# First attention of a four-layer decoder: softmax denominators moved by transfers into 128 rows of 32, and the first key and query slot loaded with the third group

## The chip, the core and the metric

The kernel runs on one core of a Trainium2 chip. The metric is the device time of one execution in microseconds (us), and the time before is the median of three runs. The core has TensorE for matrix products (PE in the views; its weight loads are PEld), VectorE (DVE), ScalarE (ACT), GpSimd (POOL) and SyncE (SP). SP computes nothing here: it issues transfers (DMAs), which the 16 DMA engines carry out. Queue q1 in the views holds the transfers that SP issues, q0 those that POOL issues.

## The reference

The reference is four layers, each an attention over a context of the same 4096 tokens and then a feed-forward block. The change touches the first attention, its preparation, and the stage that combines the first experts and prepares the second attention. With 64 batches of 64 tokens, width 256, and 8 heads of 8 rows, the first attention is

```python
qk = jnp.einsum('bdm,bdn->bmn', qh, kh) * scale
sm = jax.nn.softmax(qk, axis=-1)
ret = jnp.einsum('bmn,bcn->bcm', sm, vh)
x = x + jnp.tanh(g_xattn[0]) * _L0_xattn_ref(_layernorm(x, axis=-1), ctx_2048, ctx_2048)
```

so that the softmax runs over 256 columns of each (batch, head) pair, and its division is by one sum per row.

## The kernel before

The program is a sequence of blocks; at the end of a block all engines wait for each other. Four parts matter.

**Front** (`phase_front`). The context and x are handled in NG = 4 groups of 8 tiles of 128 tokens. For each group q, k and the normalised k are split into three bf16 pieces and stored to DRAM (`k_pieces`, `q_pieces`, `n_pieces`). SP issues these stores in order, waiting before each for the engine that made the piece. With the last group SP also loads four weight matrices (`fr_sq`), which PE transposes and ACT copies, and stores them as `turned`. At its end, SP loads slots 0 and 1 of the first attention.

**Slots** (`Slots`). A slot holds the pieces of two tiles, q and k. There are four slots; a slot's q or k is six DMAs of 768 KB in all.

**First attention** (`phase_attend` with `with_max`, the stage "a0"). It runs over 32 tiles t and 8 heads h. For tile t + 2 and head h, PE's `scores` writes the scores into one of two banks of `psM`, and DVE's `maxima` reduces the bank to row maxima (`mx`). Items (heads, and one extra per tile) take the banks in turn, and PE waits for `ring_read` before it writes a bank again. The extra item stands after head 1 of tile t + 2: `turn_and_gather(t)` transposes the maxima of tile t + 1 into the bank and, with `gather`, brings numerators and denominators of tile t - 2 into it. DVE's `shift_and_divide` then negates the maxima into two bf16 rows (`sh`), inverts the denominators (L1272, 128 x 256) and multiplies (L1274). SP's `shift(t + 1)` waits for `shift_ready` and moves `sh` in four DMAs (L1075) into two extra rows of the q slot, so that the product of q and k in `scores_t` already holds the subtraction. PE waits for all of them at head 0 of tile t + 1:

```python
if h == 0:
    if with_max:
        pe.wait_ge(shift_loaded[t % 2], 64 * (t // 2 + 1))
```

`scores_t` writes `psS` (three banks), ACT takes the exponential of each half (L1237), `values` multiplies with the context into `psV`, ACT copies that out (`ov`, L1223), and POOL adds the scaled result `res` to x. POOL also issues 36 stores of zeros to the DRAM tensor `rows_in`, one after `lay_values(t)` of each tile t, and the last five together at t = 31. After `shift(t + 1)`, SP loads q or k of a slot (L941) and, each second tile, two tiles of values (`ctl`, L1067). The semaphores of one tile and the next use alternate buffers.

**Combine** (`phase_combine_split`). In 8 groups of four tiles the expert outputs are weighed by ACT (L3374), added, normalised and split; SP loads the rows, stores the pieces, and between these loads all four slots of the second attention: k of slot i with step i of 0 to 3, q of two slots each in steps 4 and 5.

## Time and profile before

| What | us |
|---|---|
| median of three runs (lowest, highest) | 3649.17 (3646.26, 3651.99) |
| profiled execution, time | 3641.4 |
| profiled execution, span from first to last instruction | 3639.7 |
| front, from the start of the span to the first product of the first attention | 144.5 |
| first attention, from there to the first instruction of the block behind | 144.5 to 574.7 |

The span is what the trace can divide up; the profiled execution's own time is 1.7 us above it, and 7.8 us under the median. The mean granted clock of TensorE over the span is 0.887 of full speed. All times of rows are counted from the start of the span.

### The profile page before, as it was taken

Reading aid. Unit: us, or ns where it says so; the run is one execution under the profiler, and the core shown is the slowest. Engines: PE = TensorE matmul, PEld = TensorE weight load, DVE = VectorE, ACT = ScalarE, POOL = GpSimd, SP = SyncE. Lnnn points to the kernel's source line nnn. Section 1 sums busy time; section 2 is a strip of 40 time slices with the busy share of each in tenths; the row PEclk is TensorE's granted clock in tenths of the full one; section 3 lists DMA queues with packets and bytes.
Section 4 is the critical chain, followed back from the end, with each engine's and each line's share of the span. In section 5 each row is a group of like instructions: output and inputs, shape, how many; then the busy total and the mean of one; then the engine's idle time right before and its main releaser. Section 6 shows DMA issues by size and latency. Waiting matters only on the chain. (4 is left out here: it accounts for less than half of the span.)

```text
span 3639.7 us, 60306 instructions
## 1 busy us (share of the span) xinstructions
PE 2865.4 (79%) x20178; PEld 1830.7 (50%) x20178; DVE 2155.6 (59%) x4946; ACT 1480.0 (41%) x3032; POOL 1110.8 (31%) x1494
## 2 busy tenths in 40 slices
PE   5488884466699995579947798999989749999993
PEld 4233333222355553433323486454568638888782
DVE  7699993577577776634468687888868620000003
ACT  5377772155222223579935454222245211112120
POOL 3211110277233335512279542000034441111110
PEclk7599996599899998579968899999989669999996
DMA  7766643299422224858500341000044221112204
GB/s 255 204 117 119 119 103 139 91 366 363 166 81 81 79 82 123 201 97 118 101 1 1 123 150 56 1 1 1 1 141 143 92 63 57 50 54 65 72 28 139
DMA packets 261609, 386.10 MB, mean 106 GB/s; under 512 B 56865, under 2 KB 188942, under 8 KB 261056
## 3 DMA queue, kind: packets, MB, share of 16 engines
q1 hardware_dynamic: 236160, 314.07, 32.3%
q0 software_dynamic: 25152, 68.22, 5.4%
q8 instruction: 167, 2.74, 0.3%
q14 instruction: 130, 1.06, 0.1%
HBM read 227.49 MB, written 160.24 MB: 107 GB/s over the span
## 5 line engine op out<-in xcount | busy, mean ns | idle before, releaser
L3167 POOL DMA_INDIRECT rows_out<-e_out,e_tr_dest x224 | 235.5, 1051 | 870.8 <-DVE e_out L3804 504.4
L3804 DVE COPY e_out<-e_psD 128x512 f32<-128x512 f32 x40 | 27.7, 692 | 492.3 <-PE e_psD L3772 492.1
L1237 ACT ACTIVATE a_pt<-a_psS 128x512 f32<-128x512 f32 x512 | 277.6, 594 | 102.0 <-PE a_psS L1133 97.7
L1259 DVE TENSOR_REDUCE a_mx_sb<-a_psM 128x4 f32<-128x1024 f32 x256 | 293.2, 1213 | 9.2 <-PE a_psM L1116 8.2
L3572 PE MATMUL e_psG<-e_wgu,e_yT 128*128 x576 | 275.1, 600 | 25.9 <-ACT e_yT L3600 23.3
L1147 PE MATMUL a_psV<-a_pt,a_vt 128*18 128x256 f32 x4096 | 291.1, 386 | 1.2 <-issue 0.8
L3772 PE MATMUL e_psD<-e_w,e_hT 128*128 128x256 f32 x1280 | 289.9, 386 | 0.0
L3761 PE MATMUL e_psH<-e_yT,e_w 128*128 128x256 f32 x1280 | 284.9, 381 | 1.6 <-issue 0.8
L3704 ACT ACTIVATE e_hT<-e_psH 128x512 f32<-128x512 f32 x160 | 95.6, 597 | 452.6 <-PE e_psH L3761 452.6
L3761 PEld LDWEIGHTS e_psH<-e_yT,e_w 128*128 128x128 f32 x1280 | 244.4, 191 | 35.7 <-issue 2.1
L3772 PEld LDWEIGHTS e_psD<-e_w,e_hT 128*128 128x128 f32 x1280 | 245.5, 194 | 33.3
L1244 ACT ACTIVATE a_pt<-a_psS 128x1024 f32<-128x1024 f32 x256 | 241.6, 1043 | 10.7 <-PE a_psS L1133 9.9
L3606 ACT ACTIVATE e_th<-e_gcap 128x256 f32<-128x256 f32 x144 | 60.0, 417 | 332.4 <-DVE e_ucl L3640 332.4
L1133 PE MATMUL a_psS<-a_q_first,a_k_first 48*128 48x256 bf16 (+1 forms) x1536 | 144.2, 280 | 30.0 <-PEq L119 10.3
L3637 DVE TENSOR_TENSOR e_gub<-e_psG,e_bgu 128x512 f32<-128x512 f32 x144 | 99.3, 690 | 108.6 <-PE e_psG L3572 99.5
L1470 PE MATMUL kv_psK<-e_bgu,e_bd 128*128 128x512 f32 x256 | 127.8, 647 | 32.0 <-DMA e_bd<-ctxT 32.0
L3589 PE MATMUL e_psO<-e_wd,e_hT 128*128 x576 | 149.4, 382 | 2.4 <-ACT e_hT L3612 1.6
L3572 PEld LDWEIGHTS e_psG<-e_wgu,e_yT 128*128 128x128 f32 x576 | 98.9, 192 | 100.1 <-issue 99.9
L1147 PEld LDWEIGHTS a_psV<-a_pt,a_vt 128*18 128x18 f32 x4096 | 86.4, 97 | 108.9 <-issue 68.5
L2858 POOL DMA_INDIRECT rows_in<-sc_y,sc_i x128 | 129.2, 1009 | 38.5 <-issue 37.6
L1043 POOL TENSOR_TENSOR xs<-xs,a_res 128x256 f32<-128x256 f32 x64 | 46.3, 725 | 257.8 <-DVE a_res L1274 257.7
L1133 PEld LDWEIGHTS a_psS<-a_q_first,a_k_first 48*128 48x128 bf16 (+1 forms) x1536 | 54.7, 95 | 127.8 <-ACT a_pt L1244 53.7
(433 smaller groups left out, 6221.1 us busy)
## 6 DMA issues: line engine op xcount, KB each, us to landing
kbd<-e_bgu SPq DMA_DIRECT2D x64, 512.0 KB, 4.6
cr_kbd<-kbd SPq DMA_DIRECT2D x64, 512.0 KB, 3.4
rows_in<-zeros POOLq DMA_DIRECT2D x36, 522.0 KB, 6.3
e_xin<-rows_in SPq DMA_DIRECT2D x144, 128.0 KB
vbd<-e_bd SPq DMA_DIRECT2D x64, 272.0 KB, 4.0
cr_vbd<-vbd SPq DMA_DIRECT2D x64, 272.0 KB, 2.6
cq_rows<-rows_out SPq DMA_DIRECT2D x32, 512.0 KB, 12.1
e_w<-in_L_ffn_w_dram SPq DMA_DIRECT2D x16, 1024.0 KB, 7.6
```

The costliest lines, as they stand in the source:

```text
L1133: ins = pe.matmul(psS[:, (first + b) % S_BANKS, k * DIM:(k + 1) * DIM], at_tile("k", rows(b, KR), t, h, slice(k * P, (k + 1) * P)), at_til ...
L1147: ins = pe.matmul(psV[32 * q:32 * q + 2 * V, b, :], vt[:, t % 4, 2 * k + b, g, q, :], pt[:, probs(t, 4 * g + q), b, k, :], start=(g == 0 a ...
L1237: act.activation(pt[:, probs(t, h), b, :, :], psS[:, unit(t, h, b) % S_BANKS, :].rearrange("p (k c) -> p k c", k=KC), ACT.Exp, scale=scale ...
L1244: act.activation(pt[:, probs(t, h), :, :, :], psS[:, first:first + 2, :].rearrange("p b (k c) -> p b k c", k=KC), ACT.Exp, scale=scale).th ...
L1259: dve.tensor_reduce(mx[:, t % 2, :, h, :], psM[:, k % 2, :, :].rearrange("p b (f c) -> p b f c", f=2), AX_X, ALU.max).then_inc(ring_read, 1)
L1470: ins = pe.matmul(self.psK[:, u, :], self.ct[:, i % 4, k, :], self.w[:, layer, k, :], start=(k == 0), stop=(k == KC - 1))
L2858: pool.indirect_dma_start(out=rows_in[:, :], out_offset=bass.IndirectOffsetOnAxis(ap=index[u][:, k:k + 1], axis=0), in_=y[:, u, :], in_off ...
L3167: pool.indirect_dma_start(out=self.rows_out[0:limit, :], out_offset=bass.IndirectOffsetOnAxis(ap=self.dest[:, t:t + 1], axis=0), in_=rows, ...
L3572: ins = pe.matmul(psG[:, u, :], yT[:, u, k, :], wgu[:, e, k, :], start=(k == 0), stop=(k == KC - 1))
L3589: ins = pe.matmul(psO[:, u, 0:D], hT[:, u, k, :], wd[:, e, k, :], start=(k == 0), stop=(k == KC - 1))
L3761: ins = pe.matmul(psH[:, b, (f % 2) * R:(f % 2 + 1) * R], w1s[:, m, k, f * P:(f + 1) * P], yT[:, u, :, k, :], start=(k == 0), stop=(k == K ...
L3772: ins = pe.matmul(psD[:, u, tt * D:(tt + 1) * D], hT[:, u, f, tt * P:(tt + 1) * P], w2s[:, m, f, :], start=(f == 0), stop=(f == FC - 1))
```

## The change

It has three parts.

1. **First attention.** The maxima are laid out so that one transpose (32 x 128) takes the place of two (16 x 128). `sh` has 32 rows of 128 then, and `shift` needs eight DMAs where it had four. `gather` brings numerators only (two products for four), and ACT copies them to `numer`. The denominators stand in four rows per half of `ov`: `move_sums`, two DMAs, spreads them over 128 rows of 32 (`sums`), DVE inverts 128 x 32, `move_inverses`, one DMA, brings them into 16 rows of 256 (`inverse`), and one product with a matrix of ones and zeros (`repeat`) repeats each over its 8 rows. DVE multiplies. The inverse is taken one tile later than before (`INVERT_LAG`), the scaling two (`SCALE_LAG`), so two more extra items stand at the end.
2. **Front.** Slot 0 is loaded after the third group's stores, slot 1 at the start of the attention. Of the last group's normalised pieces two are stored by ACT, and so are the four `turned` matrices.
3. **Combine.** Only slots 0 and 1 are loaded there, q and k together in steps 6 and 7; slots 2 and 3 are loaded in the second attention.

```diff
+                    if g < NG - 1:
+                        for piece, n_done in enumerate((n_hi, n_mid, n_lo)):
+                            sp.wait_ge(n_done, g + 1)
+                            store_normal(sp, g, piece)
+                    if g == NG - 2:
                         for operand in ("q", "k"):
                             slots.load(sp, operand, 0)
-                    for piece, n_done in ((0, n_hi), (1, n_mid), (2, n_lo)):
-                        sp.wait_ge(n_done, g + 1)
-                        sp.dma_start(n_pieces[g, :, :, PIECES - 1 - piece].rearrange("b h d t c -> (b h) d (t c)"),
-                                     np[:, piece, :, :].rearrange("p t c -> p (t c)")).then_inc(n_stored, 16)
-                for m, (_, dst) in enumerate(pairs):
-                    sp.wait_ge(w_copied, m + 1)
-                    sp.dma_start(dst.rearrange("(k p) o -> p k o", p=P), wt[:, m, :, :]).then_inc(w_stored, 16)
-                for operand in ("q", "k"):
-                    slots.load(sp, operand, 1)
+                sp.wait_ge(n_lo, NG)
+                store_normal(sp, NG - 1, 2)
                 sp.wait_ge(ct_stored, 16 * NG)
                 for u in range(2):
                     sp.wait_ge(k_stored[u], 16 * n_store * (NG // 2))
...
+                act.wait_ge(n_hi, NG)
+                store_normal(act, NG - 1, 0)
+                act.wait_ge(n_mid, NG)
+                store_normal(act, NG - 1, 1)
+                act.wait_ge(w_copied, n_w)
+                for m, (_, dst) in enumerate(pairs):
+                    act.dma_start(dst.rearrange("(k p) o -> p k o", p=P), wt[:, m, :, :]).then_inc(w_stored, 16)
                 act.wait_ge(tanhed, 1)
...
-                        pool.wait_ge(ring_read, turn_item(t + LEAD) + 1)
+                        pool.wait_ge(ring_read, turn_item(t + SCALE_LAG) + 1)
...
-                                         sh[HEADS * b:HEADS * (b + 1), t % 2, s, :]).then_inc(shift_loaded[t % 2], 16)
-
+                            for f in range(2):
+                                rank = PAIR * f + HEADS * b
+                                sp.dma_start(at_tile("q", slice(row, row + 1), t, slice(0, HEADS), slice(f * P, (f + 1) * P)),
+                                             sh[rank:rank + HEADS, t % 2, s, :]).then_inc(shift_loaded[t % 2], 16)
+
+                def move_sums(t):
+
+                    sp.wait_ge(out_done, t + 1)
+                    if t >= 2:
+                        sp.wait_ge(inverted, t - 1)
+                    half = P // 2
+                    for g in range(2):
+                        row = V * g + HD
+                        sp.dma_start(sums[half * g:half * (g + 1), t % 2, :], ov[row:row + 97:32, t % 2, :, :]).then_inc(sums_moved, 16)
+
+                def move_inverses(t):
+
+                    sp.wait_ge(inverted, t + 1)
+                    if t >= 2:
+                        sp.wait_ge(turned, t - 2 + SCALE_LAG + 2)
+                    sp.dma_start(inverse[:, t % 2, :], rec[:, t % 2, :]).then_inc(inverses_moved, 16)
+
+                for s in range(slots.early, 2):
+                    slots.load(sp, "q", s)
+                    slots.load(sp, "k", s)
                 load_values(0)
-                load_values(1)
-                if slots.early < BUFS:
-                    slots.load(sp, "q", 2)
                 if with_max:
                     shift(0)
-                if slots.early < BUFS:
+                load_values(1)
+                slots.load(sp, "q", 2)
+                if with_max:
                     sp.wait_ge(ones_set, 1)
-                    slots.load(sp, "k", 2)
+                slots.load(sp, "k", 2)
                 for t in range(TILES):
                     if with_max and t + 1 < TILES:
                         shift(t + 1)
+                    if with_max and t >= INVERT_LAG:
+                        move_inverses(t - INVERT_LAG)
+                    if with_max and t >= LEAD:
+                        move_sums(t - LEAD)
                     s = t // 2 + 3
-                    if slots.early <= s < NS:
+                    if s < NS:
                         if s >= BUFS:
                             last = SLOT_TILES * (s - BUFS) + SLOT_TILES - 1
                             for b in range(2):
                                 sp.wait_ge(st_done[b], HEADS * (last + 1))
-                        elif t % 2:
-                            sp.wait_ge(ones_set, s - slots.early + 1)
+                        elif with_max and t % 2:
+                            sp.wait_ge(ones_set, s - 1)
                         slots.load(sp, "k" if t % 2 else "q", s)
                     if t % 2 == 0 and t // 2 + 2 < NS:
                         load_values(t // 2 + 2)
                     if t == 20 and prelude is not None:
                         prelude.load(sp)
+                if with_max:
+                    for t in range(TILES, TILES + INVERT_LAG):
+                        move_inverses(t - INVERT_LAG)
+                        if t < TILES + LEAD:
+                            move_sums(t - LEAD)
...
                         pe.wait_ge(ring_read, k - 1)
+                    if copies_before(k - 2):
+                        pe.wait_ge(numer_copied, copies_before(k - 2))
...
                     pe.wait_ge(ring_read, item(t, HEADS - 1) + 1)
-                    for f in range(2):
-                        ins = pe.transpose(bank[0:PAIR, f * P:(f + 1) * P], mx[:, t % 2, :, :, f].rearrange("p b h -> p (b h)"), core.ident[:, :])
-                    return ins
-
-                def gather(t, out):
...
 
+                def repeat_inverses(t, out):
+
+                    pe.wait_ge(inverses_moved, 16 * (t + 1))
+                    return pe.matmul(out, repeat[:, :, :, :].rearrange("r b h d -> r (b h d)"), inverse[:, t % 2, :], start=True, stop=True)
+
                 def turn_and_gather(t):
 
                     k = turn_item(t)
                     pe.wait_ge(ring_read, k - 1)
+                    if copies_before(k - 2):
+                        pe.wait_ge(numer_copied, copies_before(k - 2))
                     if t + 1 < TILES:
                         ins = turn_max(t + 1, psM[:, k % 2, 0, :])
-                    if 0 <= t - LEAD:
-                        ins = gather(t - LEAD, psM[:, k % 2, 1, :])
+                    if 0 <= t - LEAD < TILES:
+                        ins = gather(t - LEAD, psM[:, k % 2, 1, :], 1)
+                    if 0 <= t - SCALE_LAG:
+                        ins = repeat_inverses(t - SCALE_LAG, psM[:, k % 2, 0, DIM:])
                     ins.then_inc(turned, 1)
 
...
                     if t >= 2:
                         act.wait_ge(turned, t - 2 + LEAD + 2)
+                        if with_max:
+                            act.wait_ge(sums_moved, 32 * (t - 1))
                     act.activation(ov[:, t % 2, :, :], psV[:, :, :], ACT.Copy).then_inc(out_done, 1)
+
+                def copy_numer(t):
+                    act.wait_ge(turned, t + LEAD + 2)
+                    if t >= 4:
+                        act.wait_ge(ring_read, turn_item(t - 4 + SCALE_LAG) + 1)
+                    act.activation(numer[:, t % 4, :], psM[:, turn_item(t + LEAD) % 2, 1, 0:DIM], ACT.Copy).then_inc(numer_copied, 1)
...
-                def shift_and_divide(t):
-                    k = turn_item(t)
+                    dve.tensor_tensor(res[:, t % 2, :], psN[:, 0, :], rec[:, t % 2, :], ALU.mult).then_inc(scaled, 1)
+
+                def shift_and_scale(t):
+                    bank = psM[:, turn_item(t) % 2, 0, :]
                     dve.wait_ge(turned, t + 2)
                     if t + 1 < TILES:
-                        shifts(t + 1, psM[:, k % 2, 0, :])
-                    if 0 <= t - LEAD:
-                        divide(t - LEAD, psM[:, k % 2, 1, 0:DIM], psM[:, k % 2, 1, DIM:2 * DIM], ring_read)
+                        shifts(t + 1, bank)
+                    u = t - SCALE_LAG
+                    if u >= 0:
+                        if u >= 2:
+                            dve.wait_ge(added, u - 1)
+                        dve.wait_ge(numer_copied, u + 1)
+                        dve.tensor_tensor(res[:, u % 2, :], numer[:, u % 4, :], bank[:, DIM:2 * DIM], ALU.mult).then_inc(ring_read, 1)
                     else:
                         dve.wait_ge(shift_ready, t + 2)
                         dve.sem_inc(ring_read, 1)
+                    u = t - INVERT_LAG
+                    if 0 <= u < TILES:
+                        dve.wait_ge(sums_moved, 32 * (u + 1))
+                        if u >= 2:
+                            dve.wait_ge(inverses_moved, 16 * (u - 1))
+                        dve.reciprocal(rec[:, u % 2, :], sums[:, u % 2, :]).then_inc(inverted, 1)
 
                 dve.memset(psV[:, :, :], 0.0).then_inc(cleared, 1)
...
-                    if i < slots.early:
-                        slots.load(sp, "k", i)
-                    if i in (4, 5):
-                        sp.wait_ge(stored[i % 2], 16 * PIECES)
-                        for s in range(2 * i - 8, 2 * i - 6):
-                            slots.load(sp, "q", s)
+                    if i == 4:
+                        sp.wait_ge(stored[0], 16 * PIECES)
+                    if 0 <= i - 6 < slots.early:
+                        slots.load(sp, "q", i - 6)
+                        slots.load(sp, "k", i - 6)
                     if 0 <= i - 3:
                         store(i - 3, 1, mid)
                     if 0 <= i - 2 < NG:
...
         with ExitStack() as c:
-            slots = Slots(core, c, "a0", q_pieces, k_pieces, 2)
...
             held = ExitStack()
-            slots = Slots(core, held, "a1", q_pieces, n_pieces, Slots.BUFS)
```

How the order moves, at three places. On DVE, one tile in the middle of the first attention, before (`a_mx_sb` are the row maxima, `a_sh_sb` is `sh`):

```order
L1259 TENSOR_REDUCE a_mx_sb<-a_psM 128x2x2 x8
L1264 TENSOR_SCALAR a_sh_sb<-a_psM 16x256
L1266 SCALAR_TENSOR_TENSOR a_sh_sb<-a_psM,a_sh_sb 16x256
L1272 RECIPROCAL a_rec<-a_psM 128x256
L1274 TENSOR_TENSOR a_res<-a_psM,a_rec 128x256
```

and with the change:

```order
L1334 TENSOR_REDUCE a_mx_sb<-a_psM 128x4 x8
L1339 TENSOR_SCALAR a_sh_sb<-a_psM 32x128
L1341 SCALAR_TENSOR_TENSOR a_sh_sb<-a_psM,a_sh_sb 32x128
L1361 TENSOR_TENSOR a_res<-a_numer,a_psM 128x256
L1370 RECIPROCAL a_rec<-a_sums 128x32
```

The eight reductions stay; the reciprocal has an eighth of its columns and stands behind the multiplication. On SP, what is issued for one tile with an even number, before:

```order
L1075 DMA a_q_rest<-a_sh_sb 1x8x256 x4
L941 DMA a_q_first<-q_pieces 8x8x512
L941 DMA a_q_first<-q_pieces 16x8x512
L941 DMA a_q_first<-q_pieces 24x8x512
L941 DMA a_q_first<-q_pieces 8x8x512
L941 DMA a_q_first<-q_pieces 16x8x512
L941 DMA a_q_first<-q_pieces 24x8x512
L1067 DMA a_ctl<-ctxT 128x2x256
```

and with the change:

```order
L1101 DMA a_q_rest<-a_sh_sb 1x8x128 x8
L1119 DMA a_inverse<-a_rec 16x8x32
L1112 DMA a_sums<-a_ov_sb 64x1x32 x2
L949 DMA a_q_first<-q_pieces 8x8x512
L949 DMA a_q_first<-q_pieces 16x8x512
L949 DMA a_q_first<-q_pieces 24x8x512
L949 DMA a_q_first<-q_pieces 8x8x512
L949 DMA a_q_first<-q_pieces 16x8x512
L949 DMA a_q_first<-q_pieces 24x8x512
L1091 DMA a_ctl<-ctxT 128x2x256
```

Eleven DMAs now stand for the four, and the slot loads behind them. On PE, the extra item and what surrounds it, before:

```order
L1147 MATMUL a_psV<-a_pt,a_vt 18x256 x4
L1116 MATMUL a_psM<-a_k_first,a_q_first 128x256 x4
L1154 MATMUL a_psM<-ident,a_mx_sb 16x128 x2
L1161 MATMUL a_psM<-a_ov_sb,a_pick 64x256 x4
L1133 MATMUL a_psS<-a_q_rest,a_k_rest 128x256 x4
```

and with the change:

```order
L1203 MATMUL a_psV<-a_pt,a_vt 18x256 x4
L1172 MATMUL a_psM<-a_k_first,a_q_first 128x256 x4
L1209 MATMUL a_psM<-ident,a_mx_sb 32x128
L1215 MATMUL a_psM<-a_ov_sb,a_pick 64x256 x2
L1222 MATMUL a_psM<-a_inverse,a_repeat 128x256
L1189 MATMUL a_psS<-a_q_rest,a_k_rest 128x256 x4
```

Four instructions in the place of six, the last one with a wait for `move_inverses`.

## Rows read from the trace of the kernel before

**Rows 1.** Windows: busy us (instructions) per engine, TensorE clock, DMA share, GB/s.
```profile
106.00:144.50 38.50, 8.03 (x35) 6.21 (x36) 15.32 (x8) 10.09 (x10) 0.04 (x1) 0.63 0.95 274
...
200.00:529.00 329.00, 281.32 (x3676) 105.05 (x3676) 317.23 (x318) 243.06 (x453) 52.41 (x108) 1.00 0.60 113
```

**Rows 2.** Reciprocals and SP's issues: ns min/median/max; or busy us, mean ns.
```profile
L1272 DVE RECIPROCAL a_rec<-a_psM x32: 1734/1735/1759, 197.3 to 570.0; 128x256 f32<-128x256 f32 x32
...
L2750 DVE RECIPROCAL s_den<-s_den 128x32 f32<-128x32 f32 x1 | 0.4, 353 | 0.0
...
L1075 SPq DMA_DIRECT2D a_q_first<-a_sh_sb x64: 634/640/1385, 157.7 to 497.9; - x64
```

**Rows 3.** Timeline of one tile: start us, us, engine, line, [idle before, releaser].
```profile
294.29 0.39 PE L1154 MATMUL a_psM<-ident,a_mx_sb 128*16 128x128 f32 x2 [0.42 <-DVE a_mx_sb L1259]
...
295.74 0.41 DVE L1264 TENSOR_SCALAR a_sh_sb<-a_psM 16x256 bf16<-16x256 f32 x1 [0.38 <-PE a_psM L1161]
...
296.53 1.74 DVE L1272 RECIPROCAL a_rec<-a_psM 128x256 f32<-128x256 f32 x1
...
296.63 2.70 SPq L1075 DMA_DIRECT2D a_q_first<-a_sh_sb  x4
...
298.64 9.13 DVE L1259 TENSOR_REDUCE a_mx_sb<-a_psM 128x4 f32<-128x1024 f32 x8
...
299.43 3.78 SPq L941 DMA_DIRECT2D a_q_first<-q_pieces  x6
...
303.93 0.38 PE L1133 MATMUL a_psS<-a_q_first,a_k_first 50*128 50x256 bf16 x4
...
308.15 0.41 DVE L1264 TENSOR_SCALAR a_sh_sb<-a_psM 16x256 bf16<-16x256 f32 x1 [0.38 <-PE a_psM L1161]
```

**Rows 4.** DMA issues: KB each, median us from issue to landing.
```profile
cr_bq<-in_L_xattn_bq_dram SPq DMA_DIRECT2D x2, 0.5 KB, 2.2
```

**Rows 5.** Timeline near the end of the first attention, around its last zeros.
```profile
529.65 2.98 POOL L430 DMA_DIRECT2D rows_in<-zeros  x4
...
532.64 16.65 SPq L1075 DMA_DIRECT2D a_q_rest<-a_sh_sb  x8
...
540.96 0.39 PE L1133 MATMUL a_psS<-a_q_rest,a_k_rest 50*128 50x256 bf16 x4 [0.85 <-DMA a_q_rest<-a_sh_sb]
...
545.73 0.41 DVE L1264 TENSOR_SCALAR a_sh_sb<-a_psM 16x256 bf16<-16x256 f32 x1 [4.21 <-PE a_psM L1161]
```

**Rows 6.** DMA queues from 534 to 537 us: packets, MB, share; no other queue listed.
```profile
q0 software_dynamic: 263, 0.99, 101.7%
```

**Rows 7.** Windows around that stall: columns as in rows 1.
```profile
539.00:542.00 3.00, 1.50 (x24) 0.42 (x16) 2.52 (x3) 2.06 (x5) 0.00 (x0) 1.00 0.05 14
542.00:545.00 3.00, 2.96 (x20) 1.13 (x22) 0.00 (x0) 1.55 (x3) 0.00 (x0) 0.60 0.00 0
```

**Rows 8.** Timeline of the front's end.
```profile
117.27 1.97 PE L304 MATMUL fr_psN<-ident,fr_sq 128*128 128x128 f32 x16 [2.75 <-DMA fr_sq<-in_L_xattn_w_o_dram]
...
123.22 2.29 DVE L391 TENSOR_TENSOR fr_np<-fr_kn,fr_np 128x2048 bf16<-128x2048 f32 x1 [1.98 <-ACT fr_np L317]
...
140.88 2.98 SPq L941 DMA_DIRECT2D a_k_first<-k_pieces  x6
```

**Rows 9.** Timeline of ACT in the combine: the square roots of groups, and a wait.
```profile
1489.23 0.28 ACT L3381 ACTIVATE cq_nrm<-cq_psS 128x128 f32<-128x128 f32 x1 [1.21 <-PE cq_psS L3356]
...
1503.54 0.28 ACT L3381 ACTIVATE cq_nrm<-cq_psS 128x128 f32<-128x128 f32 x1 [1.21 <-PE cq_psS L3356]
...
1520.88 1.06 ACT L3399 ACTIVATE cq_parts<-cq_z_sb 128x1024 bf16<-128x1024 f32 x1 [6.87 <-DMA q_pieces<-cq_parts]
...
1540.45 0.26 ACT L3381 ACTIVATE cq_nrm<-cq_psS 128x128 f32<-128x128 f32 x1
```

**Rows 10.** Timeline of the first attention's last instructions.
```profile
566.90 0.60 ACT L1223 ACTIVATE a_ov_sb<-a_psV 128x512 f32<-128x512 f32 x1 [3.81 <-PE a_psV L1147]
...
572.33 0.72 POOL L1043 TENSOR_TENSOR xs<-xs,a_res 128x256 f32<-128x256 f32 x1 [1.40 <-DVE a_res L1274]
```

More of the change, by code:

```diff
@@ L250, in _ @@
                                    pattern=[[HD, H]], channel_multiplier=-1).then_inc(sel_made, 1)
-                for m in range(slots.early):
+                for m in range(slots.held_first):
                     pool.memset(slots.of("k", m), 1.0).then_inc(ones_set, 1)
@@ L919, in __init__ @@
         self.loaded = [core.lasting_sem(f"{name}_ql{m}") for m in range(self.BUFS)]
-        self.hold(ctx, "first", range(early), "right")
+        self.hold(ctx, "first", range(held_first), "right")
     def hold(self, ctx, part, slots, side=None):
@@ L963, in phase_attend @@
     shift_loaded = [core.sem(f"{n}_sl{m}") for m in range(2)]
-    turned, ring_read, shift_ready, hi_done = (
-        core.sem(n + k) for k in ("_tu", "_rr", "_sr", "_hi"))
+    turned, ring_read, shift_ready, hi_done, sums_moved, inverses_moved, numer_copied = (
+        core.sem(n + k) for k in ("_tu", "_rr", "_sr", "_hi", "_sm", "_im", "_nc"))
     exp_done, pv_done, out_done, gathered, v_laid, made, cleared, gated, inverted, scaled, added, ones_set = (
@@ L1002, in turn_item, with copies_before @@
             return item(TILES - 1, HEADS - 1) + 1 + t + LEAD - TILES
+        def copies_before(k):
+            return sum(1 for t in range(LEAD, TILES + LEAD) if turn_item(t) <= k)
         def unit(t, h, b):
@@ L1016, in _ @@
                 if with_max:
-                    for m in range(slots.early, BUFS):
+                    for m in range(2, BUFS):
                         pool.memset(slots.of("k", m), 1.0).then_inc(ones_set, 1)
@@ L1152, in turn_max, with gather @@
                     pe.wait_ge(ring_read, item(t, HEADS - 1) + 1)
-                    for f in range(2):
-                        ins = pe.transpose(bank[0:PAIR, f * P:(f + 1) * P], mx[:, t % 2, :, :, f].rearrange("p b h -> p (b h)"), core.ident[:, :])
-                    return ins
-                def gather(t, out):
+                    return pe.transpose(bank[0:2 * PAIR, 0:P], mx[:, t % 2, :, :, :].rearrange("p f b h -> p (f b h)"), core.ident[:, :])
+                def gather(t, out, parts):
                     pe.wait_ge(out_done, t + 1)
-                    for d in range(2):
+                    for d in range(parts):
                         for b in range(2):
@@ L1207, in _ @@
                 if with_max:
-                    turn_and_gather(TILES)
-                    turn_and_gather(TILES + 1)
+                    for t in range(TILES, TILES + SCALE_LAG):
+                        turn_and_gather(t)
                 else:
                     pe.wait_ge(scaled, TILES - 1)
-                    gather(TILES - 1, psN[:, :, :].rearrange("p d c -> p (d c)")).then_inc(gathered, 1)
+                    gather(TILES - 1, psN[:, :, :].rearrange("p d c -> p (d c)"), 2).then_inc(gathered, 1)
             @block.scalar
@@ L1245, in _ @@
                                            ACT.Exp, scale=scale).then_inc(exp_done, 2)
+                        if with_max and t >= LEAD and h == 2:
+                            copy_numer(t - LEAD)
                         if with_max and t and h == HEADS - 1:
@@ L1303, in _ @@
                             if h == 1:
-                                shift_and_divide(t)
-                    shift_and_divide(TILES)
-                    shift_and_divide(TILES + 1)
+                                shift_and_scale(t)
+                    for t in range(TILES, TILES + SCALE_LAG):
+                        shift_and_scale(t)
                 else:
```

60 lines of the change are left out of this document (38 added, 22 removed).

## The prediction

> **What bounds the kernel now.** I read the windows by stage first, then the timeline of the stage that the change rewrites, then the waits at its borders. In the first attention's steady part DVE is busy 317.23 of 329.00 us, PE 281.32 and ACT 243.06 [rows 1], so DVE is the limit. The timeline shows how closely. One tile takes from 295.74 to 308.15, 12.41 us: 2.90 for the two shift instructions, the reciprocal and the multiplication, then eight reductions in 9.13, then 0.38 in which DVE waits for PE's extra item [rows 3]. I call the start of the shift instructions T, and the start of `scores_t` for head 0 of the next tile S; here S = 303.93 = T + 8.19, and from S to the next T it is 4.22 [rows 3]. Behind DVE stands a second chain which now has slack: the shift rows. SP starts to issue them at T + 0.89, its four DMAs take 2.70 [rows 3], and a small DMA lands 2.2 after its issue [rows 4]. So they land at about T + 5.2, some 3 us before S.
>
> Outside this loop three places matter. The front ends with DMAs: DVE's last instruction ends at 125.5, SP issues until 143.9, at a DMA share of 0.95 [rows 1, 8]. Behind the first attention's last values POOL's last addition ends at 573.05 [rows 10]. In the combine, the square roots stand 14.31 apart, and then two steps take 36.91 together, in which ACT waits 6.87 for a store that SP could not issue earlier [rows 9].
>
> **The loop: what DVE gains.** The nearest row for 128 x 32 is 0.353 us, against 1.735 for 128 x 256: 1.38 saved [rows 2]. The two shift instructions have half the columns; they save at most 0.4 together, I take 0.25. PE's extra item gets shorter: from 294.29 to T it took 1.45, for two transposes and four products; now it is one transpose, two products and one more product, so I count the 0.38 wait as 0.1. DVE alone would need 12.41 - 1.38 - 0.25 - 0.3 = 10.5 per tile, and would want S at T + 6.5.
>
> ACT gains a copy of 128 x 256, under the 0.60 of the 128 x 512 copy [rows 10], and was busy 243 of 329; it has room.
>
> **The loop: what the shift rows then cost.** They are eight DMAs now, with 8 rows each as before. The row for the old ones is narrow, 634 to 640 ns for most [rows 2], and four took 2.70, so one starts 0.69 after the other. Half the bytes in each need not make an issue shorter; I take 0.69 (0.50, as for six slot loads in 2.98 [rows 8], is the other bound). The last starts 7 x 0.69 = 4.8 after the first. With the first at T + 0.65 and 2.2 to land, PE may start S at T + 7.7: 1.2 later than DVE would want it. So the chain T, eight issues, landing, S, next T becomes the limit: 7.7 + 4.2 = 11.9. From S to T I take the row's 4.22. It could be 3.6, because ACT's 0.60 copy no longer stands in front of the exponentials; it was 4.77 where PE ran at its lower clock (540.96 to 545.73 [rows 5]). Bounds from these rows are 11.3 and 12.5.
>
> SP's queue behind the shift rows matters too. `move_inverses` and `move_sums` are three more DMAs, 2.1 us, then six slot loads that took 3.78 in this tile [rows 3]. With the shift rows that is 5.5 + 2.1 + 3.8 = 11.4 us of SP's time per tile, before it waits for the next `shift_ready`; it just fits. But the slot loads, which began at T + 3.7, now begin near T + 8.2, so their data still move when the next shift rows are issued. I add 0.2 for that. The tile is then 12.1, 0.3 less than now. The trace has 28 such steps (the first reciprocal at 197.3 [rows 2], T of tile 30 at 545.73 [rows 5]): **-8.4**, and -0.8 for the stall at 540.96, which goes from there. Sums and inverses are needed a tile after they are issued; they stay hidden behind 12 us until the end.
>
> **The last zeros.** POOL lays the values of tile t + 1 and issues its zeros behind the addition of tile t - 4, which now waits for the extra item of tile t, not of t - 2. So the last five zeros are issued some 2.5 us after T of tile 30 (behind the multiplication and POOL's 0.72); before, they began ahead of T of tile 29. What they do to shift rows is in the trace: zeros from 529.65, shift rows issued from 532.64, and PE gets them at 540.96, 11.3 after the zeros [rows 5]; in between q0 moves alone [rows 6]. By that row tile 31's shift rows arrive at T + 13.8 where PE wants them at about T + 8.2: **+5.5** (bounds 0 and 7). The Trainium skill, page "DMA: Bandwidth & Descriptors", section "Queues, rings and completion order", says that each DMA engine takes turns between its queues packet by packet. By that rule the shift rows would slip in and the term be near zero, the sum 5.5 lower; the trace does not agree there, so I keep the row.
>
> **The tail.** Now reciprocal, transfer, product and multiplication follow each other for tiles 29, 30 and 31, since SP issues in order and each `move_inverses` waits for a reciprocal which waits for sums. A round is 0.35 + 2.2 + 0.4 + 0.42, the sums behind it 0.7 to 1.4 more: three rounds of 4.1, 12.3, and the addition 0.7. Before, it was 6.15 from ACT's last copy to the end [rows 10], about 0.9 of it up to the first reciprocal, so 5.3. That is +7.7, and +0.8 for two copies on ACT where ACT sets the pace: **+8.5** (6 to 12).
>
> **The front.** Twelve slot DMAs go ahead of the last group's weight loads; six took 2.98 [rows 8], so PE's product moves from 117.27 to about 123, DVE's last split from 123.22 to 129.2, and it ends at 131.5. Then ACT still issues six stores, 3 us at 0.50 each. The block ends at about 135 instead of 144.5. Bounds: -5.6, if data and not issues set the end (slot 1's 1.5 MB at 274 GB/s [rows 1]), and -12. I take **-9**. Slot 1 and the first shift rows then share the DMAs with the first zeros: **+0.5**.
>
> **The combine.** Without loads in steps 0 to 5 the two long steps should be 14.31 each: 36.91 - 28.6 = 8.3. The 24 DMAs in steps 6 and 7 meet fewer row loads; I take **-7** (0 to -10). The second attention needs slot 2 only four tiles in.
>
> Sum: -8.4 - 0.8 + 5.5 + 8.5 - 9 + 0.5 - 7 = -10.7. From the profiled execution's 3641.4 that is 3630.7; the median shown is 7.8 above it, 3649.2 - 10.7 = 3638.5.
>
> **Rivals.** (A) The above, a tile of 11.5 to 12.5: 3638, own range 3620 to 3652. Chance 0.55.
> (B) Issues of half-width rows are shorter, about 0.5 or less; then they land by T + 6.5 and DVE stays the limit at 10.5: 28 x 1.9 = 53 gained in place of 8.4, 3594. For it speaks that slot loads of far more bytes issue in 0.50 [rows 8]; against it the same: bytes do not set the price, and these DMAs keep their 8 rows. Chance 0.12 (3594 to 3620).
> (C) PE loses its clock in the new wait. Between 539 and 542 PE was busy 1.50 of 3.00 us, waiting for shift rows; from 542 to 545 its granted clock was 0.60, so most of that at the level of 1.2 GHz, and DVE idled 4.21 [rows 5, 7]. In the steady part it was 1.00, 2.4 GHz [rows 1]. With a wait of 1.2 us and another for the first exponential in every tile this can recur in every tile: 7.7 + 4.8 + 0.5 = 13.0, 0.6 more than now, +17 for the loop, 3664. From 12.7 per tile on the kernel is slower. Queued slot data would act at the same place. Chance 0.23. The Trainium skill, page "TensorE: Matmul & The Clock Gate", section "HAM oscillation — how this bites in real kernels", describes this: waits for DMAs between bursts throttle PE again, and every next burst starts cold. The two windows here agree with it once; whether it repeats no row shows.
> (D) Front and combine give back nothing (their stores wait for the same data later): 3654. Chance 0.10.
>
> A measurement of this kernel can tell about 0.2%, 7.3 us, from no change: faster is below 3641.9, slower above 3656.5. Two thirds of A and all of B are faster: 0.50. Slower is most of C and some of D: 0.21. The rest is 0.29. The range 3600 to 3664 leaves out the far half of B and the upper part of C.
>
> **What would show it.** The step between two reciprocals (128 x 32, about 0.35) should be near 12.1; PE's wait at `scores_t` should name `a_sh_sb` in most tiles, DVE's idle time should come before the reduction of head 0. If no wait names it and the step is 10.5, B holds. If the granted clock in the steady part is well under 1.00, C. The block of the attention should begin near 135, the stage behind it about 12 to 14 us later than the loop's gain alone would say, and the combine's square roots stand 14.3 apart throughout. The prediction is wrong if an issue is not 0.69, or if 4.22 does not carry over from S to T.

## The result, and the profile after

The changed kernel takes 3691.12 us (median of five runs), the one before 3649.17; the ratio is 1.0103, 95% interval 1.0085 to 1.0121. It is slower, and above the range that was predicted. One of its five runs took 4243.84 us at a granted clock of 0.678, and one of the twelve of experiment 2 took 5095.24 at 0.548; the ratios leave both out. The profile here is of the same kernel run again beside the experiments (3698.9 us, span 3697.2; ratio 1.0084, interval 1.0071 to 1.0097). As in the prediction, T is the start of the shift instructions and S the start of `scores_t` for head 0. A step is the time from one T to the next. "27 steps" below are those from the fourth T to the thirty-first, 335.3 us before (12.42 each) and 357.6 now (13.25).

Its timeline: the front's end, three tiles of the loop, the tail.

```profile
128.61 3.27 PE L305 MATMUL fr_psN<-ident,fr_sq 128*128 128x128 f32 x16 [15.65 <-DMA fr_sq<-in_L_xattn_w_o_dram]
...
134.38 2.29 DVE L399 TENSOR_TENSOR fr_np<-fr_kn,fr_np 128x2048 bf16<-128x2048 f32 x1 [14.69 <-ACT fr_np L318]
134.95 5.96 ACTq L363 DMA_DIRECT2D turned<-fr_kr  x4
...
491.23 0.28 DVE L1339 TENSOR_SCALAR a_sh_sb<-a_psM 32x128 bf16<-32x128 f32 x1 [0.45 <-PE a_psM L1222]
...
491.85 5.84 SPq L1101 DMA_DIRECT2D a_q_first<-a_sh_sb  x8
...
493.38 0.77 POOL L438 DMA_DIRECT2D rows_in<-zeros  x1
...
498.80 0.39 PE L1189 MATMUL a_psS<-a_q_first,a_k_first 50*128 50x256 bf16 x4 [0.33 <-DMA a_q_first<-a_sh_sb]
...
500.16 2.37 SPq L949 DMA_DIRECT2D a_q_rest<-q_pieces  x6
...
502.57 0.92 SPq L1091 DMA_DIRECT2D a_ctl<-ctxT  x1
502.61 0.28 DVE L1339 TENSOR_SCALAR a_sh_sb<-a_psM 32x128 bf16<-32x128 f32 x1
...
503.53 5.64 SPq L1101 DMA_DIRECT2D a_q_first<-a_sh_sb  x8
...
513.92 0.61 PE L1189 MATMUL a_psS<-a_q_first,a_k_first 50*128 50x256 bf16 x4 [4.07 <-DMA a_q_first<-a_sh_sb]
...
519.92 0.28 DVE L1339 TENSOR_SCALAR a_sh_sb<-a_psM 32x128 bf16<-32x128 f32 x1 [1.20 <-PE a_psM L1222]
...
569.27 3.76 POOL L438 DMA_DIRECT2D rows_in<-zeros  x5 [0.18 <-issue]
...
581.13 0.61 PE L1189 MATMUL a_psS<-a_q_rest,a_k_rest 50*128 50x256 bf16 x4 [7.41 <-DMA a_q_rest<-a_sh_sb]
...
599.15 0.60 ACT L1288 ACTIVATE a_ov_sb<-a_psV 128x512 f32<-128x512 f32 x1 [3.80 <-PE a_psV L1203]
...
612.74 0.72 POOL L1067 TENSOR_TENSOR xs<-xs,a_res 128x256 f32<-128x256 f32 x1 [3.28 <-DVE a_res L1361]
```

The tile from 491.23 is what was predicted: eight shift rows in 5.84, S at T + 7.57, next T 3.81 behind it, 11.38 in all. In the next tile the same eight rows come at T + 11.31, 3.7 later, and the tile takes 17.31, although SP issues them as fast (5.64). In 13 of the 27 tiles the rows come later than T + 7.9. Steps of 11.6 or less are 6 of the 27, steps over 12.8 are 16. The windows of the same places (columns as in [rows 1]):

```profile
200.00:529.00 329.00, 288.72 (x3326) 99.89 (x3322) 259.75 (x293) 230.82 (x443) 43.98 (x92) 0.89 0.60 111
...
502.60:511.00 8.40, 7.25 (x104) 2.40 (x102) 7.98 (x10) 7.21 (x14) 1.92 (x4) 1.00 0.90 165
511.00:514.00 3.00, 0.08 (x2) 0.08 (x4) 0.21 (x1) 0.00 (x0) 0.00 (x0) 0.94 0.45 97
514.00:517.00 3.00, 2.74 (x24) 0.77 (x24) 1.23 (x1) 2.17 (x4) 0.00 (x0) 0.50 0.85 133
517.00:520.00 3.00, 3.00 (x14) 1.03 (x11) 1.31 (x2) 0.00 (x0) 0.00 (x0) 0.50 0.52 53
520.00:524.00 4.00, 4.00 (x36) 1.16 (x32) 2.29 (x5) 2.45 (x5) 1.91 (x4) 0.52 0.16 57
```

In the steady part the granted clock is 0.89 where it was 1.00. In this tile PE, idle for four microseconds, comes back at half clock (1.2 GHz) and has it for ten; in that time PE is the busy engine and DVE waits. What moves while the rows are awaited, by queue (packets, MB, share of the 16 DMA engines), first from 503.6 to 506.6, then from 509.6 to 511.6, and last the issue of the values in the stretch before (its us from issue to landing at the end):

```profile
q1 hardware_dynamic: 414, 0.39, 97.5%
q0 software_dynamic: 9, 0.04, 3.6%
...
q0 software_dynamic: 80, 0.29, 42.3%
q1 hardware_dynamic: 278, 0.04, 12.6%
...
a_ctl<-ctxT SPq DMA_DIRECT2D x1, 256.0 KB, 8.1
```

Slot data and values, issued from 500.16 to 503.49 in the same queue, fill the DMA engines first; the 2 KB rows stand behind them, and when they move, the zeros' queue q0 has the larger share. Two price rows and the combine's square roots:

```profile
L1370 DVE RECIPROCAL a_rec<-a_sums x32: 332/333/352, 209.7 to 608.6; 128x32 f32<-128x32 f32 x32
...
L1101 SPq DMA_DIRECT2D a_q_first<-a_sh_sb x128: 634/635/1336, 154.3 to 525.7; - x128
...
L3465 ACT ACTIVATE cq_nrm<-cq_psS x8: 277/278/278, 1506.9 to 1600.1; 128x128 f32<-128x128 f32 x8
```

### The profile page after: what moved, and what is told of

Read it like the earlier page. It is cut to its first block and busy times, and to the rows that moved or that the text cites. A ratio compares the mean times of both kernels' runs of the same rounds, so it can differ in the third digit from the quotient of the medians.

```text
span 4242.1 us, 60731 instructions
## 1 busy us (share of the span) xinstructions
PE 3596.0 (85%) x20082; PEld 2027.9 (48%) x20082; DVE 2129.3 (50%) x4946; ACT 1513.7 (36%) x3064; POOL 1092.1 (26%) x1496
## 5 line engine op out<-in xcount | busy, mean ns | idle before, releaser
L3656 PE MATMUL e_psG<-e_wgu,e_yT 128*128 x576 | 380.3, 798 | 3.4 <-issue 3.1
L3845 PE MATMUL e_psH<-e_yT,e_w 128*128 128x256 f32 x1280 | 372.0, 463 | 1.5 <-ACT e_yT L3783 0.8
L3856 PE MATMUL e_psD<-e_w,e_hT 128*128 128x256 f32 x1280 | 370.9, 462 | 0.0
L1203 PE MATMUL a_psV<-a_pt,a_vt 128*18 128x256 f32 x4096 | 363.9, 468 | 0.8 <-issue 0.8
L3845 PEld LDWEIGHTS e_psH<-e_yT,e_w 128*128 128x128 f32 x1280 | 263.6, 206 | 102.7 <-issue 2.1
L1555 PE MATMUL kv_psK<-e_bgu,e_bd 128*128 128x512 f32 x256 | 192.3, 927 | 31.4 <-DMA e_bd<-ctxT 31.4
L3673 PE MATMUL e_psO<-e_wd,e_hT 128*128 x576 | 201.8, 487 | 0.5 <-ACT e_hT L3696 0.5
L2538 PE MATMUL bs_psU<-bs_wu,bs_yT 128*128 128x512 f32 x256 | 151.4, 748 | 0.0
L2500 PE MATMUL bs_psG<-bs_wg,bs_yT 128*128 128x512 f32 x256 | 150.9, 745 | 0.0
L1189 PE MATMUL a_psS<-a_q_first,a_k_first 50*128 50x256 bf16 (+1 forms) x1024 | 114.4, 321 | 32.2 <-DMA a_q_first<-a_sh_sb 10.8
```

The costliest lines, as they stand in the source:

```text
L1203: ins = pe.matmul(psV[32 * q:32 * q + 2 * V, b, :], vt[:, t % 4, 2 * k + b, g, q, :], pt[:, probs(t, 4 * g + q), b, k, :], start=(g == 0 a ...
L1555: ins = pe.matmul(self.psK[:, u, :], self.ct[:, i % 4, k, :], self.w[:, layer, k, :], start=(k == 0), stop=(k == KC - 1))
L2500: ins = pe.matmul(psG[:, c, :], yT[:, t % 3, k, :], wg[:, k, c * 512:(c + 1) * 512], start=(k == 0), stop=(k == KC - 1))
L2538: ins = pe.matmul(psU[:, c, :], yT[:, t % 3, k, :], wu[:, k, c * 512:(c + 1) * 512], start=(k == 0), stop=(k == KC - 1))
L3656: ins = pe.matmul(psG[:, u, :], yT[:, u, k, :], wgu[:, e, k, :], start=(k == 0), stop=(k == KC - 1))
L3673: ins = pe.matmul(psO[:, u, 0:D], hT[:, u, k, :], wd[:, e, k, :], start=(k == 0), stop=(k == KC - 1))
```

## The experiments

Each is compared with the kernel before on the same chip. The first expectations name three theories of the loss. Theory 1 is the chain of eight issues, with PE at full clock. Theory 2 is PE's lower clock: steps of 13.0 to 13.8 and a granted clock clearly under 1.00. Theory 3 is the borders of the loop: front, last zeros, tail and combine.

**1. The parts apart.** One kernel has parts 2 and 3 of the change alone, one part 1 alone.

> Kernel before with parts 2 and 3 of the change alone (front, slot loads, combine); the attention's arithmetic as before. If the prediction's terms for the borders hold (front -9, combine -7, first slots +0.5), it takes 3634 us, 0.996. If the borders give nothing back, 3649. If the loss lies in the borders (theory 3), above 3665.

> Part 1 of the change alone (the attention's arithmetic and its transfers); front, slot loads and combine as before. With theory 1 or 2 the whole loss is here: 3649 + 45 + what the borders give, 3690 to 3705. With theory 3 about 3654 (the prediction's loop, zeros and tail: -8.4 - 0.8 + 5.5 + 8.5 = +4.8).

Parts 2 and 3: ratio 0.9964 (0.9951 to 0.9977), a gain of 13 us by the ratio and 8 by the medians; its trace shows 6, the attention ending 1.0 later and the combine 7.4 shorter. Part 1: 1.0101 (1.0087 to 1.0115), the whole loss; its 27 steps sum to 356.2. The windows of the steady part, parts 2 and 3 first:

```profile
200.00:529.00 329.00, 281.14 (x3668) 104.94 (x3664) 317.22 (x318) 243.09 (x454) 53.08 (x108) 1.00 0.61 113
```
```profile
200.00:529.00 329.00, 285.32 (x3312) 98.51 (x3309) 260.01 (x293) 230.35 (x442) 43.99 (x92) 0.90 0.60 111
```

**2. Eight transfers in the kernel before.**

```diff
-sp.dma_start(at_tile("q", slice(row, row + 1), t, slice(0, HEADS)), sh[..., t % 2, s, :])
+for f in range(2):
+    half = slice(f * P, (f + 1) * P)
+    sp.dma_start(at_tile("q", slice(row, row + 1), t, slice(0, HEADS), half), sh[..., t % 2, s, half])
```

> Kernel before with each of the four shift transfers of a tile cut into two of half the columns, nothing else changed. Theory 1 with 0.69 us per issue: the rows land at T + 0.9 + 4.8 + 2.2 = T + 7.9, 0.3 before S = T + 8.2, so the loop stays near 12.4 and the kernel within 10 us of before. If the eight transfers take longer than that (issues of 0.8 us or more, or landing above 3 us), the tile grows by the excess, 3665 us or more. Theory 2 (clock through a wait for shift rows) would show as a granted clock under 1.00 here too, if the rows come late.

1.0014 (1.0001 to 1.0028). The timeline of a usual tile shows the eight issues, the zeros, and an unchanged step of 12.40:

```profile
402.48 0.41 DVE L1266 TENSOR_SCALAR a_sh_sb<-a_psM 16x256 bf16<-16x256 f32 x1 [0.38 <-PE a_psM L1163]
...
403.36 5.41 SPq L1077 DMA_DIRECT2D a_q_first<-a_sh_sb  x8
...
411.17 0.77 POOL L430 DMA_DIRECT2D rows_in<-zeros  x1
414.88 0.41 DVE L1266 TENSOR_SCALAR a_sh_sb<-a_psM 16x256 bf16<-16x256 f32 x1 [0.38 <-PE a_psM L1163]
```

Eight issues alone cost little in the loop: of the 27 steps, 26 are unchanged within 0.3 us and one is 15.58, where the rows come at T + 10.40; their sum is 338.5, 3 more than before. Here the slot loads follow at T + 6.4, and a tile of 12.4 gives the data 1 us more to pass; that this is what protects it is my reading, not shown.

**3. Zeros.** In the changed kernel POOL issues each tile's zeros at T + 2.15, amid the shift rows; before it was T + 8.7. The prediction had seen this only at the end. Three kernels: the changed one with `pool.wait_ge(pv_done, lump(t - 2, 1, 1) + 1)` ahead of the zeros; the one before with `pool.wait_ge(shift_ready, t + 1)` there; the changed one with all zeros behind the last addition.

> The changed kernel, with one more wait on POOL: zeros of tile t are issued behind the values of tile t - 2, so at about T + 8 as before the change, not at T + 2.15 in the middle of the shift rows. Zeros theory: the shift rows land at T + 7.6 in nearly every tile, steps are 11.4 us (the changed kernel's undisturbed ones) in place of 11.4 to 15.4, granted clock in the steady part near 1.00, about 28 x 1.8 = 50 us less than the changed kernel: 3646 us, 0.997 of before. Rival, the slot data alone (768 KB behind eight issues, issued from T + 8.6 and ahead of the next shift rows in the same queue): the long steps stay at 13 to 15 us and the time within 10 us of the changed kernel's.

> The kernel before, with one more wait on POOL that puts the zeros of each tile behind the shift instructions (T + 0.9 to T + 1.5 in place of T + 8.7). Zeros theory: the four shift rows (issued T + 0.9 to T + 3.6) are held up by the zeros' 0.5 MB; the slot data are done by then, so they land near T + 7.5 to 8.5 where T + 8.2 is wanted: some steps of 12.4 grow to 13 or more, the kernel 5 to 25 us slower than before. Rival (zeros harmless, slot data alone): no change, 12.41 throughout.

> The changed kernel with all 36 stores of zeros issued by POOL behind its last addition of the first attention; the block behind pays for them, so only the attention's part of the trace is read. Zeros theory: steps 11.4 or less from the third tile on, last shift rows at T + 7.6 in place of T + 14.4. Slot theory: long steps stay in the tiles with slot loads.

Late zeros: 1.0055 (1.0036 to 1.0073), but the 27 steps still sum to 352.7; the gain is mostly at the end, where the last rows come at T + 7.21 and not T + 14.25, because the last five zeros are now issued behind them, at T + 8.0. Early zeros in the kernel before: 0.9996 (0.9979 to 1.0013), 27 steps 335.4; that kernel's rows have slack, so this alone would not clear the changed one. No zeros in the loop: 27 steps 337.2, 9 still over 12.8 (the block behind pays for them, 3724.39 us in one run). Moving the zeros gives the loop back 5 us, taking them out 20: their place is not the main cause, but as bytes they are part of it. In the late-zeros kernel, one of the long tiles, and its last rows and zeros:

```profile
472.85 0.74 SPq L949 DMA_DIRECT2D a_q_rest<-q_pieces  x2
473.63 0.38 SPq L1093 DMA_DIRECT2D a_ctl<-ctxT  x1
473.71 0.28 DVE L1341 TENSOR_SCALAR a_sh_sb<-a_psM 32x128 bf16<-32x128 f32 x1 [0.38 <-PE a_psM L1224]
...
483.85 0.39 PE L1191 MATMUL a_psS<-a_q_first,a_k_first 50*128 50x256 bf16 x4 [2.90 <-DMA a_q_first<-a_sh_sb]
...
567.54 0.39 PE L1191 MATMUL a_psS<-a_q_rest,a_k_rest 50*128 50x256 bf16 x4 [0.37 <-DMA a_q_rest<-a_sh_sb]
...
568.34 3.75 POOL L438 DMA_DIRECT2D rows_in<-zeros  x5 [5.80 <-issue]
```

The zeros of the long tile are issued at T + 7.25, and its rows come at T + 10.14 all the same.

**4. The bytes ahead of the rows.** From slot 4 on, each slot load brings one head of eight. The other seven keep the data of an earlier slot, so this kernel leaves out part of the result and serves as a test only.

```diff
+heads = slice(0, 1) if self.name == "a0" and s >= self.BUFS else slice(0, HEADS)
-eng.dma_start(tensor[at:at + HD * run, place, :, :, :]...
+eng.dma_start(tensor[at:at + HD * run, place, heads, :, :]...
```

> The changed kernel, in which the slot loads of the first attention from slot 4 on bring one head of eight (the same number of transfers, an eighth of the bytes; the other heads keep the data of an earlier slot, so the output is not the reference's). Slot-data theory (the shift rows' packets queue behind 0.75 MB of slot data and 0.25 MB of values that still move when they are issued): from slot 4 on no rows land after T + 7.8, steps are 11.3 to 11.5 us in place of 11.4 to 15.4, PE's clock in the steady part near 1.00, 3697 - 27 x 1.5 = 3655 us. Rival (issues and PE's clock alone, no matter what the queue holds): the long steps stay and the time is within 10 us of 3697.

3650.49 us in one run, its kernel before 3650.86. The 27 steps sum to 324.8, 17 of them 11.6 or less and 8 over 12.8, the clock 0.95; a few rows still come late, up to T + 8.55. A quiet tile:

```profile
430.91 0.28 DVE L1340 TENSOR_SCALAR a_sh_sb<-a_psM 32x128 bf16<-32x128 f32 x1
...
438.50 0.39 PE L1190 MATMUL a_psS<-a_q_rest,a_k_rest 50*128 50x256 bf16 x4 [0.35 <-DMA a_q_rest<-a_sh_sb]
...
442.31 0.28 DVE L1340 TENSOR_SCALAR a_sh_sb<-a_psM 32x128 bf16<-32x128 f32 x1
```

Of the 50 us by which the 27 steps exceed 27 x 11.38, the slot bytes carry 33 (357.6 - 324.8) when they alone are cut, and the zeros 20 (357.6 - 337.2) when they alone are taken out. The two sum to more than 50: presumably a row that stands behind both comes early when either goes. Each is from one run.

**5. Four transfers.** The maxima's layout, `turn_max`, `shifts` and `shift` as before, all else as changed; then the late zeros with it.

```diff
-mx = core.sb(ctx, n + "_mx_sb", [P, 2, 2, 2, HEADS], F32)
-sh = core.sb(ctx, n + "_sh_sb", [2 * PAIR, 2, 2, P], BF16)
+mx = core.sb(ctx, n + "_mx_sb", [P, 2, 2, HEADS, 2], F32)
+sh = core.sb(ctx, n + "_sh_sb", [PAIR, 2, 2, DIM], BF16)
```

> The changed kernel with the maxima laid out as before, so two transposes and four shift transfers of 8 x 256 in place of one and eight of 8 x 128; zeros where the change has them. The last issue starts 2.1 us after the first and not 5.1, the rows land at T + 4.8 where nothing disturbs them, and slot loads are issued by T + 8 as the sums set them. If eight issues are the cause, steps fall to DVE's 10.8 and the kernel to 3697 - 28 x 2.4 = 3630 us. If the zeros are the cause whatever the number of rows, long steps stay, but from an earlier base: landing at T + 7 to 7.5, steps of 10.8 to 12.5, 3650 to 3665 us.

> The changed kernel with four shift transfers (as in the run before) and with the zeros of tile t behind the values of tile t - 2. The only long step left in the four-transfer kernel (15.5 us) and the wait for the last rows should go: 11.42 throughout, 0 to 8 us under the four-transfer kernel's 0.9953 of before, so about 0.994. If late zeros meet the slot loads in their place (T + 7.2 and T + 6.1), steps of 12 or more come back and it is no faster than the four-transfer kernel.

0.9953 (0.9935 to 0.9971), and 0.9915 (0.9894 to 0.9935) with late zeros: both beat the kernel before. The 27 steps sum to 311.9 and 318.8, with one and four over 12.8. A tile of the first:

```profile
393.37 0.41 DVE L1339 TENSOR_SCALAR a_sh_sb<-a_psM 16x256 bf16<-16x256 f32 x1 [0.56 <-PE a_psM L1222]
...
394.26 2.78 SPq L1099 DMA_DIRECT2D a_q_rest<-a_sh_sb  x4
...
400.75 3.48 DVE L1334 TENSOR_REDUCE a_mx_sb<-a_psM 128x4 f32<-128x1024 f32 x3 [0.25 <-PE a_psM L1170]
...
404.79 0.41 DVE L1339 TENSOR_SCALAR a_sh_sb<-a_psM 16x256 bf16<-16x256 f32 x1 [0.56 <-PE a_psM L1222]
```

It takes 11.42, as long as an undisturbed tile with eight transfers and not the 10.8 expected, but no PE wait for rows is in it: DVE works 10.6 and waits 0.25 and 0.56 for PE. The gain over eight transfers is slack, not speed.

**6. PE ahead of the wait.** In two kernels `scores(t + LEAD, 0)` stands ahead of `scores_t(t, 0)`: the changed one, and the one with four transfers and late zeros.

> The changed kernel with PE's scores of head 0 of tile t + 2 written ahead of scores_t of head 0 of tile t, so ahead of the wait for the shift rows, not behind it. DVE then has one more reduction (1.2 us) to do while the rows are late, and PE is busy for 0.6 us more before the wait. If the price of late rows is DVE's idle time, each long step gets shorter by up to 1.2 us: 3697 - 14 x 1.2 = 3680 us; more if PE then keeps its higher clock. If PE's own chain behind the wait (scores_t, exponentials, values at the lower clock) sets the step, it stays within 5 us of 3697.

> Four shift transfers, late zeros and scores ahead of the wait together, as a version that may beat both kernels: steps 11.0 to 11.4 us, 3620 to 3632 us, 0.992 to 0.995 of before. If PE's order costs what it gives (scores_t of head 0 is 0.4 us later in every tile where the rows are early), it is slower than four transfers with late zeros by up to 10 us.

1.0108 (1.0088 to 1.0128), no gain, 27 steps 360.2: one more reduction for DVE while the rows are late does not shorten the loop, so DVE's idle time was not the price. With four transfers 0.9921 (0.9903 to 0.9939), 27 steps 307.8, none over 11.65; the same as without it.

**7. Lateness or clock.** Of the 50 us, 21 are rows later than T + 7.6 (in 13 tiles, not 12); the rest stands in the stretches at half clock behind them. Eight of the 13 waits, of 1.53 to 4.07 us, are followed by such a stretch within 3 us; five, of 0.73 to 1.31, are not. In tiles 4 to 30 PE repeats `scores_t`'s products ahead of the wait, three or five times.

```diff
+pe.wait_ge(exp_done, first + 2 - S_BANKS)
+for _ in range(3):
+    ... pe.matmul(psS[:, (first + b) % S_BANKS, ...], ..., start=True, stop=True)
```

> The changed kernel, with filler on PE: in tiles 4 to 30, ahead of the wait for the shift rows, PE repeats the products of scores_t of head 0 (without the two shift rows) three times, 12 products, about 1.2 us; their result is overwritten. Nothing else changes. Where rows arrive at T + 7.6 the filler makes PE about 0.9 late, so by itself it costs 27 x 0.9 = 24 us less what the late tiles hide (12 x 0.9), +13 us. Clock theory (of the loop's excess of 50 us over 11.38 a tile, 29 come from PE's lower clock after waits of over 1.2 us, not from the wait itself): shorter idle stretches keep the clock, the 13 us tiles without a wait go, steps near 12.3, the 27 steps sum to 335 to 345 in place of 357, kernel 5 to 20 us faster than the changed one. Lateness theory: clock and 13 us tiles stay, 27 steps sum to about 370, kernel 13 us slower.

> As the run before, with five repeats, about 2.1 us of filler, so that PE starts scores_t of head 0 at about T + 9.4 in every tile and only rows later than that make it wait. Clock theory: granted clock in the steady part 1.00, scores_t of head 0 to the next T is 3.8 us in nearly every tile, steps a flat 13.2, 27 steps 356 to 362 us, the kernel as fast as the changed one within 6 us although PE has 57 us more work. Lateness theory: the excess behind late tiles stays on top, 27 steps sum to 375 or more, 20 us slower.

1.0079 (1.0065 to 1.0094) and 1.0090 (1.0073 to 1.0108); 27 steps 356.7 and 359.3; the clock stays at 0.90 and 0.92. The filler was smaller than I had counted, 20 products in 1.25 us, so an undisturbed tile grew by 0.16 and 0.6 only, and the sums of both theories lie closer together than their expectations say: the runs do not decide between them. With five repeats, the timeline and windows of one tile:

```profile
402.45 1.25 PE L1185 MATMUL a_psS<-a_q_first,a_k_first 48*128 48x256 bf16 x20
...
404.98 0.39 PE L1197 MATMUL a_psS<-a_q_first,a_k_first 50*128 50x256 bf16 x4 [1.27 <-DMA a_q_first<-a_sh_sb]
```
```profile
404.90:407.90 3.00, 2.46 (x24) 0.72 (x24) 1.23 (x1) 2.17 (x4) 0.00 (x0) 0.74 0.79 142
405.40:405.90 0.50, 0.19 (x4) 0.00 (x0) 0.18 (x1) 0.49 (x1) 0.00 (x0) 1.00 0.82 227
405.90:406.40 0.50, 0.34 (x6) 0.13 (x6) 0.50 (x1) 0.50 (x2) 0.00 (x0) 0.92 1.03 154
406.40:406.90 0.50, 0.50 (x10) 0.15 (x8) 0.50 (x1) 0.50 (x2) 0.00 (x0) 0.50 0.77 109
407.90:410.50 2.60, 2.60 (x11) 0.95 (x11) 1.23 (x1) 0.00 (x0) 0.00 (x0) 0.50 0.87 106
410.50:414.50 4.00, 4.00 (x35) 1.25 (x36) 2.37 (x5) 2.45 (x5) 1.91 (x4) 0.50 0.31 66
```

Here PE comes back at full clock (its four products take 0.39, and took 0.61 at half clock in the tile at 513.92), waits 0.47 more for ACT, and falls to half clock 1.3 us after it came back. Even a wait cut to 1.27 us behind 1.25 us of work is followed by half clock: a little filler does not hold it. That the clock costs its 29 us by itself is read from the windows from 407.90 on, in which PE is busy throughout at 0.50, and not shown by a run.

## Why the prediction was wrong

Times are of the two profiled executions, before to after; a part of the sum at a time.

| Step | predicted | measured |
|---|---|---|
| loop, third T to the last (361.4 to 379.9), with the stall | -9.2 | +18.4 |
| first slots and rows, first T to the third (27.5 to 33.3) | +0.5 | +5.8 |
| last zeros, last T to S of tile 31 (6.8 to 14.25) | +5.5 | +7.5 |
| tail, from there to POOL's last addition (20.6 to 32.3) | +8.5 | +11.8 |
| front, start of the attention (144.5 to 141.4) | -9 | -3.1 |
| combine, first to last square root (100.6 to 93.2) | -7 | -7.4 |
| sum | -10.7 | +33.0 |

At the last multiplication of the second attention the two executions are 39.1 us apart (1839.0 and 1878.1); 6 more than the sum, which arise between the first attention and the combine, in stages that the change doesn't touch. Behind it they drift apart by another 18, which the medians, 42 apart, don't confirm.

**What DVE gains** was right in DVE's work and not in the tile: the reciprocal takes 0.333 and DVE works 10.6 in a tile, but the undisturbed tile with four transfers takes 11.42 and not 10.5, because DVE waits 0.56 for PE's extra item (predicted 0.1) and 0.25 for scores.

**What the shift rows cost** was right for a tile with an empty queue: issues of 0.635, S at T + 7.57 (predicted 7.7), then 3.81 (4.22), 11.38 (11.9). The step that failed is "their data still move when the next shift rows are issued. I add 0.2 for that." Over the 27 steps it was 50.3 / 27 = 1.9: the rows come late in 13 of 27, up to 3.7 us (0.8 a step), and PE loses its clock behind them (1.1 a step), for which the sum had nothing. Nor had it a term for each tile's zeros, which the change moves amid the rows. In the quiet tile PE already waits 0.33 for the rows, which land at T + 7.57, so no slack is left, where the kernel before had 3 us by the prediction's estimate. Cutting the slot bytes (experiment 4) takes 33 of the 50 us away, four transfers (5) 46.

**Rival C** is what happened, with 13.25 for its 13.0. It had the right two causes, the clock and the queued slot data, at 0.23. That the numbers lie so close is partly luck: it priced the same loss into every tile, and the measured mean is over steps from 10.77 to 17.31. Its time, 3664, was too low above all by the front (6 us), the first rows (5) and the tail (3). The Trainium skill's page "TensorE: Matmul & The Clock Gate", section "HAM oscillation — how this bites in real kernels", says that waits between bursts bring the clock down again and again; the trace agrees, with 0.50 behind eight of the thirteen late rows. I gave it too little because the trace of before showed it once [rows 7], but there the rows had slack and here they have none. B did not come true: issues of half the bytes take as long as in [rows 2]. D did not either: front and combine give back 10.5.

**The last zeros** went by the row. PE gets its rows at T + 14.25 (predicted 13.8), and at T + 7.21 where the last zeros are issued behind them (experiment 3).

**The tail.** From ACT's last copy to the end it took 5.55 and takes 13.7, +8.2, as counted. What was left out is 3.6 us more from S of tile 31 to that copy, and after the wait of 7.41 PE starts at half clock there too (0.61 for the four products).

**The first slots and rows** were priced at 0.5 and cost 5.8: the second T's rows come at T + 13.74, and still at T + 13.43 with all zeros out of the loop. Slot 2's loads stand just ahead of them in SP's queue; that these hold them up is not shown.

**The front.** The step that failed is "Twelve slot DMAs go ahead of the last group's weight loads; six took 2.98, so PE's product moves from 117.27 to about 123": I counted issues, and the twelve took 5.8 us as I had counted, but the weights arrive at 128.6, not 123, and DVE's last split starts at 134.38, not 129.2. That the slots' data decide is my reading; no run moves them alone. ACT then issues the four `turned` matrices in 5.96, where the prediction had 2, and that sets the end of the block. The bound of -5.6 by data was the better guide, and still too far. Slot 1 at the attention's start then costs part of it again: with parts 2 and 3 alone the attention starts 3.9 us earlier and ends 1.0 later.

**The combine** was right. The square roots stand 13.3 us apart on average, without a long step.

## What to carry to other kernels

When a change speeds up the engine that is the bound, list what else has a deadline in the loop, and how far ahead of it it is now; here a chain with some 3 us of slack was lengthened by 2.4 us while its deadline moved nearer, and the mean over quiet tiles said nothing of the tiles in which a full queue stands ahead of it. Small transfers with a deadline should be few, and nothing large should be issued shortly ahead of them in their queue; where they must be many, keep the layout that needs fewer. Price a late transfer as its lateness plus PE's restart at half clock, more than twice the lateness here (50 us for 21).

## What the hardware showed that was not expected

A transfer of eight half rows takes SP as long to issue as one of eight whole rows (median 0.635 us for 2 KB and 0.640 for 4 KB). PE's clock fell to half after an idle stretch of as little as 1.27 us, with 1.25 us of products just ahead of it: not at once, but 1.3 us after PE had come back. In the long tile of the first timeline it then stayed at half for ten. Where the zeros of a tile are issued, amid the rows or 7.5 us later, made no difference to the kernel before (0.9996), though in the changed kernel their last five together hold up the last rows by 7 us.
